# Channel products over tiles of 128 tokens, the last tile in strips, and a new order of work in a metaformer layer

## What is computed

```python
# per image, after a layer norm over channels
theta, phi = relu(bn(th_w @ x)), relu(bn(ph_w @ x))          # 32 x 784
Gs = theta^T phi                                             # 784 x 784, folded into "mix"
ys = concat([mean(relu(bn(gxs_w @ x))), relu(bn(ggs_w @ [Gs^T, Gs]))])
x  = sigmoid(bn(ws2_w @ relu(bn(ws1_w @ ys)))) * x           # gate of each token
# channel attention: weights contract over the 784 tokens
theta_c, phi_c, g_c = relu(bn(thc_w @ xc)), relu(bn(phc_w @ xc)), relu(bn(gxc_w @ xc))   # 196 x 128 each
x  = x_in + sigmoid(...theta_c, phi_c, g_c...) * x           # gate of each channel
# layer norm, router over 8 experts, top 2, experts 128 x 128
t  = t + sum_k p_k * (expert_w[e_k] @ ln(t))
```

## Time and profile before

| what | value |
|---|---|
| median of 3 runs | 1913.96 us (1911.57 to 1919.20) |
| profiled execution | 1912.15 us, its span 1910.1 us |
| PE, PEld, DVE, ACT, POOL busy | 96, 70, 79, 61, 59% |
| mean granted TensorE clock | 0.992 |
| DMA | 135.1 MB, mean 71 GB/s |

### The profile page before, as it was taken

One profiled execution on the slowest core, in us unless ns is written; L12 is line 12 of the kernel. 1 busy time (PEld: TensorE's weight loads), 2 busy tenths in 40 slices (PEclk: granted clock), 3 DMA queues, 4 the chain that ended last, 5 costly groups with the idle time before them and its releaser, 6 DMA issues.

```text
span 1910.1 us, 39142 instructions
## 1 busy us (share of the span) xinstructions
PE 1834.2 (96%) x13396; PEld 1342.4 (70%) x13396; DVE 1505.3 (79%) x4697; ACT 1174.2 (61%) x3240; POOL 1128.1 (59%) x1233
## 2 busy tenths in 40 slices
PE   4889999999999999999999999999999999999996
PEld 3567777777777777767777777777777777776774
DVE  5368878878888888887878888887888887887666
ACT  4446665656665666666665666565666566666544
POOL 2236556656556757556666655666655675755465
PEclk9899999999999999999999999999999999999998
DMA  4111212121222121222211122212121212121111
GB/s 130 51 69 61 77 69 86 69 80 49 77 69 86 69 86 52 76 70 77 82 73 66 63 77 69 86 69 74 55 77 69 86 69 86 52 69 60 44 52 51
DMA packets 43344, 135.10 MB, mean 71 GB/s; under 512 B 7980, under 2 KB 9597, under 8 KB 43150
## 3 DMA queue, kind: packets, MB, share of 16 engines
q1 hardware_dynamic: 42488, 130.78, 19.5%
q10 hardware_dynamic: 662, 1.84, 0.3%
HBM read 106.50 MB, written 26.10 MB: 69 GB/s over the span
## 4 chain that ended last, share of the span: by engine, by line
PE 61%; ACT 19%; DVE 8%; POOL 7%; issue 3%; DMA 1%; SPq 1%; ACTq 0%; POOLq 0%; DVEq 0%
ACT part L746 9%; PE rot L999 4%; PE rot L979 4%; PE rot L1043 4%; PE rot L1044 4%; PE rot L1053 4%; ACT j L618 4%; PE high L1188 4%; PE low L1188 3%; POOL x1l L517 3%; PE high L1189 3%; PE high L1190 3%; PE rot L1141 3%; PE rot L1179 3%; PE rot L915 3%
## 5 line engine op out<-in xcount | busy, mean ns | idle before, releaser
L1613 DVE SCALAR_TENSOR_TENSOR part<-high,gv,part 128x128 f32<-128x128 f32 (+1 forms) x1664 | 463.4, 341 | 129.1 <-ACT part L746 116.8
L746 ACT ACTIVATE part<-low,gv 128x128 f32<-128x128 f32 (+1 forms) x1664 | 467.8, 375 | 142.1 <-POOL otok L530 73.0
L525 POOL TENSOR_TENSOR part<-part 128x256 f32<-128x256 f32 (+1 forms) x416 | 341.3, 820 | 283.3 <-DVE part L1613 279.4
L530 POOL TENSOR_TENSOR otok<-part 128x128 f32<-128x128 f32 (+1 forms) x416 | 281.7, 677 | 32.6
L1043 PE MATMUL rot<-x1h,wch 112*128 112x256 f32 x1120 | 278.1, 286 | 0.7 <-ACT chan L693 0.7
L1044 PE MATMUL rot<-x1h,wcl 112*128 112x256 f32 x1120 | 272.5, 281 | 0.0
L500 POOL TENSOR_TENSOR tp_l<-tp,tp_h 128x448 fp32r<-128x448 f32 x64 | 71.8, 1122 | 268.5 <-ACT tp_h L632 268.5
L1043 PEld LDWEIGHTS rot<-x1h,wch 112*128 112x128 f32 x1120 | 212.1, 189 | 6.1 <-issue 1.1
L1044 PEld LDWEIGHTS rot<-x1h,wcl 112*128 112x128 f32 x1120 | 212.6, 190 | 1.4
L1188 PE MATMUL low<-weh,xh 128*128 128x512 f32 (+1 forms) x416 | 180.2, 433 | 6.3 <-ACT part L746 5.1
L517 POOL TENSOR_TENSOR x1l<-tok,x1h 112x1024 fp32r<-112x1024 f32 x64 | 136.0, 2126 | 84.5 <-ACT x1h L686 84.5
(11 more groups left out here) (225 smaller groups left out, 3754.3 us busy)
## 6 DMA issues: line engine op xcount, KB each, us to landing
xin<-in_x SPq DMA_DIRECT2D x32, 784.0 KB, 4.3
y_ch<-rstd_rows SPq DMA_DIRECT2D x32, 784.0 KB, 4.0
x<-in_x SPq DMA_DIRECT2D x32, 784.0 KB, 4.3
cen<-shift_rows SPq DMA_DIRECT2D x32, 784.0 KB, 4.1
out<-x SPq DMA_DIRECT2D x64, 392.0 KB, 2.4
otok<-in_ggs_w SPq DMA_DIRECT2D x1, 600.2 KB
tok<-in_ggs_w SPq DMA_DIRECT2D x1, 600.2 KB
rstd_rows<-both_rows SPq DMA_DIRECT2D x32, 6.1 KB
```

Source lines behind the costliest of these rows:

```text
L525: nc.gpsimd.tensor_tensor(part[0:n, slot, 0:2, :], part[0:n, slot, 0:2, :], part[0:n, slot, 2:4, :], ALU.add).then_inc(sem("half_sum"), 1)
L530: nc.gpsimd.tensor_tensor(otok[0:n, i, :], part[0:n, slot, 0, :], part[0:n, slot, 1, :], ALU.add).then_inc(sem("token_ready"), 1)
L746: last = nc.scalar.activation(part[0:n, turn % RING, e, :], low[turn % 2][0:n, e * C:(e + 1) * C], ACT.Copy, scale=gv[par(p, back)][0:n, i ...
L1613: last = nc.vector.scalar_tensor_tensor(out=own, in0=high[turn % 2][0:n, e * C:(e + 1) * C], scalar=gv[par(p, back)][0:n, i, HALF + e:HALF ...
```

## The change

First half. Tokens are now in tiles of 128: six whole ones (WHOLE) and a last one that holds the last 128 tokens (from REST = 656), of which only the last 16 are new; `valid` masks the others. All `tok`, `st1`, `rstd1`, `gain`, `wch` and `x1h` grow to 128 partitions. The three products of the last tile become one matmul: `wrest` and the seventh tile of `x1h` hold the high and low halves in strips of partitions. `x1_high(1)` is four ACT copies for it (five for both calls), `x1_low(1)` two POOL subtractions with a wait between. `to_channels` turns the last tile with one transpose of 32 rows. The trip of rstd has two DMAs back instead of one. `gx` is one call of four matmuls into four strips of 32 partitions of one bank.

Order. USES and the step lists of PE, ACT, DVE and POOL are new. SP issues 5 instead of 12 of `wide` ahead of the first rstd row and the expert weights in turn 1; ACT issues `big` behind the first token copies.

```diff
                 def x1_high(g, back):
...
-                        nc.scalar.copy(x1h[:, lo:hi, :, :], tok[third(k, p, back)][:, lo:hi, :, :]).then_inc(sem("x1_hi_ready"), 1)
+                        last = nc.scalar.copy(x1h[:, lo:min(hi, WHOLE), :, :], own[:, lo:min(hi, WHOLE), :, :])
+                        if hi > WHOLE:
+                            nc.scalar.copy(x1h[64:128, WHOLE, :, :], own[64:128, WHOLE, :, :])
+                            for r in (0, 32):
+                                last = nc.scalar.copy(x1h[r:r + 32, WHOLE, :, :], own[96:128, WHOLE, :, :])
+                        last.then_inc(sem("x1_hi_ready"), 1)
...
                 def x1_low(g, back):
...
+                        last = nc.gpsimd.tensor_tensor(x1l[:, lo:min(hi, WHOLE), :, :], own[:, lo:min(hi, WHOLE), :, :],
+                                                       x1h[:, lo:min(hi, WHOLE), :, :].bitcast(F32), ALU.subtract)
+                        if hi > WHOLE:
+                            last.then_inc(sem("x1_full_ready"), 1)
+                            need(pool, "x1_full_ready", k, p, 1, back)
+                            last = nc.gpsimd.tensor_tensor(x1h[96:128, WHOLE, :, :], own[96:128, WHOLE, :, :],
+                                                           x1h[96:128, WHOLE, :, :].bitcast(F32), ALU.subtract)
...
                 def channel_low(m, back):
...
-                        for j in range(lo, hi):
-                            last = nc.tensor.matmul(dst, wch[:, j, rows], x1l[:, j, :, :].rearrange("p b c -> p (b c)"),
-                                                    start=False, stop=(j == NT - 1))
-                    return last
+                        for j in range(lo, min(hi, WHOLE)):
+                            nc.tensor.matmul(dst, wch[:, j, rows], x1l[:, j, :, :].rearrange("p b c -> p (b c)"),
+                                             start=False, stop=False)
+                    return nc.tensor.matmul(dst, wrest[:, rows], x1h[:, WHOLE, :, :].rearrange("p b c -> p (b c)"),
+                                            start=False, stop=True)
...
                 def to_channels(use, src, b, q, back):
...
+                    dst = bank(use, k, p, back)
+                    if q == 1:
+                        nc.tensor.transpose(dst[:, S - 544:S - 512], src[96:128, WHOLE, b, :], ident[96:128, 96:128])
+                    for j in range(QUART[q][0], min(QUART[q][1], WHOLE)):
+                        last = nc.tensor.transpose(dst[:, (j - QUART[q][0]) * 128:][:, 0:128], src[:, j, b, :], ident[:, :])
...
-                def gx(q, back):
+                def gx(back):
...
+                        for b, q in PIECES:
+                            strip = slice(32 * (2 * b + q), 32 * (2 * b + q) + 32)
+                            last = nc.tensor.matmul(bank("gx", k, p, back)[strip, 0:width(q)], w3[:, 2 * IC:3 * IC],
+                                                    y_ch[:, b, cols(q)], start=True, stop=True)
```

More of the change, by code:

```diff
@@ L767, in step @@
                     wide_weights(1)
+                gate_low(7, 5)
                 gate_low(8, 5)
-                gate_low(9, 5)
-                x1_high(0, 3)
-                gate_low(10, 5)
                 x_tokens(0, 0, 1)
@@ L775, in step @@
                 x_tokens(1, 1, 1)
+                gate_low(9, 5)
+                gate_low(10, 5)
+                theta_phi(1, 2)
+                x1_high(0, 3)
+                tp_high(1, 2)
+                if 2 * k + p == 2:
+                    wide_weights(2)
                 shift_copy(4)
+                tp_tokens(1, 2)
+                if 2 * k + p == 2:
+                    wide_weights(3)
                 x1_high(1, 3)
@@ L793, in step @@
                     wide_weights(4)
+                gate_low(11, 5)
+                gate_low(12, 5)
+                channels(0, 3)
                 x_high(0, 4)
@@ L1638, in step @@
                 stats2(3, 4)
+                gate_high(6, 5)
+                moments2(4)
                 x1_tokens(0, 3)
-                moments2(4)
+                stats1(0, 1)
+                finish(1, 5)
                 gate_high(7, 5)
```

344 lines of the change are left out of this document (177 added, 167 removed).

## The result

| kernel | median | range | ratio to before, 95% interval |
|---|---|---|---|
| before | 1915.66 us | 1911.57 to 1919.20, 4 runs | |
| after | 1961.07 us | 1958.27 to 1965.58, 4 runs | 1.0237, 1.0219 to 1.0256 |

A forecast was written before the change was run, and what follows sets the result against it. PE's order was taken as the bound before, and a ring through ACT, POOL and PE after (57.7 us). Profiled 1912.15 + 26.6 (turns) - 5.6 (start) - 3 (ramps) gave 1930.2; with 1.8 for the median, 1932 us, range 1915 to 1950.

The forecast's parts named there:

- PE's own work, 53.8 us a turn: PE's matmuls, transposes, shape changes and small waits in one steady turn: 53.8 us, against a period of 56.76 before.
- that rival: On PE, the four gx strips run one after the other: +0.7 us a turn, 1952 us, chance 0.03.
- ACT reaches x1_high(0) later: On ACT, x1_high(0) comes after token copies, gate_low(10) and theta_phi(1), ending 13.6 us behind theta/phi.
- POOL's stretch of 19.9 us: POOL from x1_high(0)'s end to the last token tile: 19.9 us without a gap, 3.4 of it held up by DVE.
- DVE's centre at 29.3 or later: DVE's last centre before logits ends 29.3 us or later behind theta/phi, instead of 26.8, against 27.9 for PE.
- The way back, 24.1 us: PE from finish(3) to the next theta/phi: 24.1 us, where it was 26.2.
- 28 turns x 0.95 = 26.6: 28 full turns, each 0.95 us longer (period 57.7 on 56.76): +26.6 us.
- The start, -5.6: At the start, DVE's 11.05 us wait for the last small weight shrinks as wide weights issue later: -5.6 us.
- The ramps, -3: In turns 3 and 4 and in the drain, PE's smaller sum of work is worth 3 us.
- No contention (0.28): POOL not held up by DVE, PE's order stays the bound: period about 54.6, 1845 us, chance 0.28.
- The clock (0.07): PE's stands of 2 us twice a turn lower its clock: up to 1.7 us a turn, 1975 us, chance 0.07.
- A full lock (0.08): DVE blocks POOL fully between x_low(0) and tile 12: 1.5 us a turn more, period 59.2, 1973 us, chance 0.08.

The follow-up runs named there:

- the split kernel: After, with POOL's inverse_std1(1), x_low(0, 4) later, ACT's router_exp(4) behind joint_c(3), DVE's centre_tokens(0, 1) behind route_gates(4), centre_tokens(1, 1) behind finish(3, 5): 1877.73 us.
- the kernel of 1906.14 us: After, with POOL's inverse_std1(1) and x_low(0, 4) behind add_token(12, 5) and DVE's two centre_tokens behind route_gates(4): 1906.14 us, 0.9947 of before.
- the second experiment: After, with DVE's two centre_tokens moved to right behind or beside the four centre, gates and finish(2, 5) ahead of them: 2057.58 us, 1.0735 of before.
- the split kernels: The split kernel, 1877.73 us, and the same with the weights' issue and first wide_weights places at the start as before, 1873.60 us.
- The work alone: Work of after, but step lists, order of the banks and issue at the start as in the kernel before: 1978.46 us, 1.0315 of before.
- the work alone without the last tile's steps: The work alone, with ACT's three casts and POOL's subtraction for the last tile left out in every turn but the first: 1913.81 us, 0.9986 of before.
- DVE's moves on the kernel before: The kernel before, with DVE's centre_tokens(0, 1) behind route_gates(4) and centre_tokens(1, 1) behind finish(3, 5): 1904.06 us, 0.9935 of before.
- 1951.76: After, with POOL's inverse_std1(1) and x_low(0, 4) behind add_token(12, 5) and DVE's two centre_tokens moved behind centre(3, 4): 1951.76 us, 1.0177 of before.
- the 2005.61 us kernel: After, with one move on DVE: the two centre_tokens stand behind route_gates(4), where POOL is idle: 2005.61 us, 1.0466 of before.
- 1873.60: The split kernel with the issue of the start and the weights' places as before: 1873.60 us, 0.9771 of before.
- 1920.16: The 1873.60 us kernel with shift_turn(4) behind low_half(12, 5) on PE: 1920.16 us, 1.0023 of before.

## Why the prediction was right in its sign and short in its size

- **PE's own work, 53.8 us a turn: right.** After is busy for 1119.90/1200 of 58.00, 54.1; the split kernel's 54.0 says the same. The waits of one turn, 1.68 at `logits` and 1.59 at `finish(3)`, are about the 4 us in two parts that were forecast. The gx strips lie beside each other (0.95 us for all four, L1000), so that rival is out.
- **ACT reaches x1_high(0) later: right.** Its end was put at 13.6 us behind theta/phi; POOL could start at 823.36, that is at 13.5.
- **POOL's stretch of 19.9 us: right, 19.6, in its two parts too.** In the kernel of 1906.14 us the stretch without the pow and x_low(0) took 15.6 us. Of this 2.1 is the one add that was held up (2.84 in place of 0.73), and 0.6 is x1_low(0): in the new order it runs beside DVE's `x1_tokens(1)`, two operands in SBUF, and takes 3.02 us, here and in after, where it took 2.40:

```profile
823.36 3.02 POOL L544 TENSOR_TENSOR x1l<-tok,x1h 128x1024 fp32r<-128x1024 f32 x1 [1.10 <-ACT x1h L730]
```

  Without these 2.7, and with 2.6 and 1.0 added back, POOL needs 16.5, the forecast's own figure, and DVE cost it 3.1, where 3.4 was taken. The rule of the Trainium skill that the prediction weighed ("SBUF — State Buffer", "SBUF: two separate sides") holds in kind: the other engine is fully blocked. By its sum it overstates after, where all 4.9 us would be added and 3.1 were, and understates the second experiment, where one add lost 4.0 us to six instructions: it speaks of a whole instruction, the rows of that experiment show a whole run of them.
- **DVE's centre at 29.3 or later: right,** 29.8 (839.68).
- **The way back, 24.1 us: short by 0.6.** From `finish(3)` at 843.12 to 867.86 it is 24.7. Less the 0.4 that the way there was shorter, this makes the period 58.00 instead of 57.7. Which term of the way back was short was not looked into.
- **28 turns x 0.95 = 26.6: mis-sized.** The 28 from number 3 to the last cost 1.28 each, 35.7 us. Besides the way back, two turns were longer by 0.4 and 1.5; the latter is the one in which the clock fell.
- **The start, -5.6: the step that failed.** I had put DVE's wait for the small weights down to the 1.6 MB ahead of them. The row of after that answers to the earlier trace rows is

```profile
24.34 0.28 DVE L1376 TENSOR_SCALAR chan<-chan,cen 96x128 f32<-96x128 f32 x1 [10.90 <-DMA cen<-in_ws_b]
```

  The wait is 10.90 instead of 11.05. The transfers moved away from it were not what it waited for, and the first weight item came 1.3 later. Up to theta/phi number 1 the change costs 8.5 us (61.87 to 70.34) instead of giving 5.6. The new order of issue has a part in it, 3.0 in the pair that differs in it and in the place of the first `wide_weights` alone (67.30 and 70.34) and 0.8 in the same pair of the split kernels (66.88 and 67.67). The work alone brings number 1 to 65.0, the new lists with the old start to 67.3.
- **The ramps, -3: wrong in sign.** From number 1 to number 3 it is 1.8 us more (99.67 to 101.51), in the drain 0.4. A part of this and of the start is TensorE's clock. From 30 to 140 us, before and then after, in the same view as above:

```profile
30.00:90.00 60.00, 52.23 (x394) 34.05 (x392) 33.60 (x93) 33.10 (x78) 15.06 (x8) 0.91 0.19 63
90.00:140.00 50.00, 42.34 (x363) 31.86 (x360) 28.35 (x80) 24.49 (x54) 18.28 (x12) 0.97 0.18 66
```

```profile
30.00:90.00 60.00, 45.98 (x303) 27.88 (x302) 29.41 (x79) 35.91 (x92) 11.03 (x8) 0.74 0.21 64
90.00:140.00 50.00, 42.69 (x337) 31.39 (x337) 29.22 (x85) 22.45 (x48) 15.46 (x10) 0.93 0.19 65
```

  TensorE's clock was at the lower level for (0.09 x 60 + 0.03 x 50)/0.5 = 14 us of this before, and for (0.26 x 60 + 0.07 x 50)/0.5 = 38 us after. 24 us more at half speed are up to 12 us lost. What such time costs here, two kernels show that have the same instructions up to 118 us, the work alone and the work alone without the last tile's steps, from 65 to 118 us (the work alone first):

```profile
65.00:118.00 53.00, 45.17 (x312) 29.12 (x311) 19.86 (x57) 21.61 (x46) 10.49 (x6) 0.84 0.16 58
65.00:118.00 53.00, 43.79 (x337) 29.58 (x333) 24.15 (x73) 25.47 (x53) 11.65 (x7) 0.94 0.16 58
```

  The first was at the lower level for (0.16 - 0.06) x 53/0.5 = 10.6 us more, and its number 2 came 4.7 us later (0.5 of it was there at number 1). But the clock is not the whole of it. By the windows of 30 to 140 us every kernel with the new work was at the lower level for 27 to 38 us, DVE's moves on the kernel before for 17. Number 3 came at 161.5 before and at 161.0 with those moves, and at 166.2 to 171.8 in all the others. Among these it does not follow the clock closely: 166.9 with 34 us at the lower level in one, 168.8 with 27 in another. So a kernel with the new work is 4.6 us later at least, and how much of the 10.3 of after is work, lists or clock is not parted. Why TensorE stands longer in the first turns is argued, not shown: each weight block now takes two more activations on ACT and one more operation on DVE.
- **The rivals.** No contention (0.28) falls by POOL's rows. The clock (0.07) was given for the steady part, where it fell in one turn only; its mechanism came in the ramp, which I had counted as a gain, and in four of the experiments (0.95 to 0.98 of the steady part). By its own terms its time is 1980, not 1975. A full lock (0.08) would have been 59.2 a turn. The rival I did not have was that the work costs more than it saves until the lists of the other engines make room for it: ACT's and POOL's steps for the last tile, +0.9 and +0.3 us by my count, cost 2.0 us of period in the old order, since other engines hang on them.

So of the missing 28.4 us (46.4 against 18), 9.1 are the 28 turns (26.6 forecast, 35.7 measured), 14.1 the start (-5.6 and 8.5), and 5.2 the ramps (-3 and 2.2).

## What to carry to other kernels

Where PE is at 96%, a saving on PE is worth only what the next engine's margin allows: count the margins of the others at each place where PE meets them, and what small steps the change adds there, before counting the matmuls. When POOL and DVE both work in SBUF, place DVE's runs of two-SBUF-operand operations where POOL is idle, and keep them short: the same work was 1951.76 or 1906.14 us by the place of two of them alone, and one add took 4.83 us beside six and 2.84 beside four. That it helps to break such a run with operations that read PSUM is argued from after, not tested by itself. After a new order look at the granted clock again, in the ramp too: a wait of 2.7 us in one piece cost 1.7 or 3.4 us more behind it, turn about.

## What the runs showed of the hardware

- One POOL instruction of 0.72 us took 4.73 beside a run of six DVE instructions with two SBUF operands, 2.84 beside a run of four. One DVE instruction of 0.95 us took 4.57 beside a run of four on POOL. Beside the four `centre` of after the two engines took turns instead, and both were slowed. The Trainium skill ("SBUF — State Buffer", "Who interferes with whom") says that issue order decides who blocks. In the case of the 4.57 us POOL had begun first; in the second experiment POOL's add had begun first by its row, by 0.16 us, and still was the one that waited. (The same in the kernel of 1906.14 us, by 0.25 us. POOL's rows are the roughest of the profile, so it may have asked later than its row says.)
- The granted clock fell after a single stand of TensorE of 1.63 us in 26 of 27 turns (3.4 us at 1.2 GHz), after one of 2.71 us in every turn (3.4 and 6.9 us, turn about), and after two stands of 1.68 and 1.59 with work between in one turn of 27. Turns with the same work and the same waits show its price: 56.44 and 57.82 us. The Trainium skill ("TensorE: Matmul & The Clock Gate", "HAM oscillation — how this bites in real kernels") tells of a kernel that loses its clock in each gap of a loop; the 2005.61 us kernel does so in each turn, by waits for POOL instead of for a DMA.
- One transpose that starts 0.3 us later behind theta/phi (12.8 instead of 12.6) moved the meeting of two queues and cost 46.6 us (1873.60 to 1920.16), with no dependency broken.
